# Latent attention: keys and queries projected by unrotated and rotated dimensions, not by halves of the heads

## The chip, the cores and the metric

One core of one Trainium2 chip runs the whole program. The time is that of one execution on the device in microseconds (us); lower is better. The kernel before was timed three times, and an execution of it was recorded by the hardware profiler.

## What is computed

The input is 16 sequences (batches) of 512 tokens with 256 features. After a layer norm, a state-space block (Mamba) and a transformer block run side by side and their outputs are added. The change lies in the transformer block's attention. It has 16 heads of 16 dimensions; the first 8 dimensions of each key and query head are unrotated, the last 8 are rotated by position:

```python
kv_lat = xn @ W_kvd                  # 256 -> 64
q_lat = xn @ W_qd                    # 256 -> 64
k = (kv_lat @ W_ku).reshape(B, S, NH, HH)          # NH = 16, HH = 8
q = (q_lat @ W_qu).reshape(B, S, NH, HH)
v = (kv_lat @ W_vu).reshape(B, S, NH, HD)          # HD = 16
q_rope = (q_lat @ W_ropeq).reshape(B, S, NH, HH)
k_rope = (xn @ W_ropek).reshape(B, S, NH, HH)
k_rope = k_rope * cos + rotate_half(k_rope) * sin
q_rope = q_rope * cos + rotate_half(q_rope) * sin
kk = jnp.concatenate([k, k_rope], axis=-1)
qq = jnp.concatenate([q, q_rope], axis=-1)
scores = jnp.einsum('bqhd,bkhd->bhqk', qq, kk) * scale      # causal, softmax
y = jnp.einsum('bhqk,bkhd->bqhd', probs, v).reshape(B, S, H)
return y @ W_o
```

Behind the attention come a residual sum, a norm, a shared expert and seven routed experts of which each token takes two.

## The kernel before

Three programs run one after the other on the core: `build_attn` (norm, attention, shared expert and routing, batch by batch), `build_experts` and `build_mamba`. The change touches `build_attn` and the host's weight layouts.

**Rounds and slots.** `build_attn` is a pipeline over batches. Every engine walks through one hand-written list, `ORDER`, once a round. The spine of the list is `S2_ITEMS`, 62 items (slots 0 to 61): transposed scores with their exponentials (`s2`), products with the values (`pv`), and copies of the outputs (`oc`). `AT` puts all other items in front of a slot: n, kind, i, j. `STAGE` says which batch an item works on: in round n, `s2` works on batch n, `s1` (scores for the row maxima) on n + 1, the projections (`T`, `lat`, `kq`, `split`, `mid`, `keep`, `stack`) on n + 2, and output projection, second norm and shared expert (`wo`, `h2`, `ht`, `route`, `g`, `u`) on n - 1. Rounds run from -3 on; ten of them lie in a hardware loop of five iterations with two rounds each, the others are written out. Engines execute their items in the list's order and wait for semaphores; a wait holds up all that stands behind it on the same engine or on SyncE's queue.

**Keys and queries.** `kq` items make float32 products of 512 columns in PSUM (PE L806 to L813). Group g holds the heads 8g to 8g + 7 with all 16 dimensions, laid out dimension first, so one tile of 128 rows has unrotated rows (0 to 63) and rotated rows (64 to 127). For each group: (g, 0) adds three products, the key up-projection from the latent and the two halves of the rotary key; (g, 1) is two products, the same with the halves of each rotated head exchanged; (g, 2) and (g, 3) are the query and the exchanged query, one product each. That is 7 a group, 14 a batch. DVE multiplies each bank by a table (`rope`, cosine or signed sine; 1 and 0 in the unrotated rows; L645, L647) into `ra` and `rb`, POOL adds them into `kq` (L492).

**Three bf16 parts.** Each group's key and query (128x1024) are split into three bf16 parts: `split` rounds on ACT (L581) and subtracts on POOL (L499), `mid` does the same again (L585, L506). `keep` stores the parts of a group in DRAM (L376, 768 KB), and `stack` (group 0, slots 36 to 43) and `stack1` (group 1, slots 1 to 8 of the next round) load them back as the operands `kst` and `qst`, six pairs of transfers of 128 KB a group (L385). `s1` of the first four head pairs waits for group 0's transfers, that of the last four for group 1's.

**Banks.** PSUM has rings of two banks each: X for `s2`, Y for `s1`, Z for every other product. A product waits until its bank has been read. DVE reads Y (row maxima, L619) and most of Z; ACT reads X (exponentials, L546).

**What stands near.** `wo` (slots 25 to 31, PE L910) needs `ym1`, POOL's multiplication of the outputs by the softmax shares (L510, slot 20). POOL ends `wo` with the sum `xs` (L520). SyncE's queue has, in this order: `xload` (18), `keep` 0 (30), `xrload` (33), the stack transfers of group 0 (36 to 43) with `so` between them (39), `sl` (43), `keep` 1 and `ro` (49), `rl` (53), `nmt` (56). `so`, `sl`, `ro`, `rl` take the softmax sums through DRAM; between `sl` and `ro` DVE makes a reciprocal (`rp`, slot 48, L666). DVE then has `u` (L756), the split of the row maxima (`nm`), the ranking (`rank`) and the second `g` (L752) before the transposes of the maxima on PE (`nmt`, slot 56, L889) find their bank free.

## Time and profile before

| | |
|---|---|
| median of 3 runs | 4080.77 us (4069.5 to 4081.09) |
| the profiled execution | 4091.09 us, span 4089.3 us |
| PE (matmul) busy | 3649.6 us, 89% |
| DVE busy | 2936.9 us, 72% |
| ACT busy | 2505.8 us, 61% |
| POOL busy | 2193.6 us, 54% |
| mean granted TensorE clock | 0.954 |

The page divides the span into 40 slices of 102 us and gives each engine's busy share in tenths. The attention program takes the first 14, the experts the next 5, the Mamba block the rest. A "granted clock" of 1.00 is 2.4 GHz and one of 0.50 is 1.2 GHz; a stretch's value is the mean. PE is the matmul engine, DVE the vector engine, ACT the scalar engine, POOL GpSimd, SPq the queue of SyncE, which issues the DMAs. A float32 product of 512 columns appears as two matmul records; matmuls are pipelined, so the duration of one includes its way through the array.

### The profile page before, as it was taken

The numbers are of one execution on the slowest core, as the hardware profiler recorded it, in microseconds if no ns is written. First come the engines' busy times: TensorE is split into PE (matmuls) and PEld (weight loads), VectorE is DVE, ScalarE is ACT, GpSimd is POOL, SyncE is SP. The second block draws the span as 40 slices with busy tenths as digits, with TensorE's granted clock in tenths as the row PEclk, the third lists the DMA queues.
The fourth block names the chain that finished last, engine by engine and source line by source line (L and its number), as shares of the span: only waits on it lengthen the run. The fifth ranks groups of instructions, "written<-read, shape, count | busy, mean of one in ns | idle before, by whom it ended". The sixth has DMA issues, their size and how long they took to land.

```text
span 4089.3 us, 70514 instructions
## 1 busy us (share of the span) xinstructions
PE 3649.6 (89%) x22264; PEld 2745.8 (67%) x22264; DVE 2936.9 (72%) x5456; ACT 2505.8 (61%) x6505; POOL 2193.6 (54%) x1115
## 2 busy tenths in 40 slices
PE   5999999999999659998799999999999999899987
PEld 2455555545554447777588888888888888888776
DVE  3566555565555122222699999999999999999997
ACT  1445444454444213332678788787888878888773
POOL 3244344334442200000487787877878788787774
PEclk8899999999999779999899999999999999999998
DMA  4333342333332157666222122221222222122221
GB/s 113 98 93 113 93 120 88 104 107 112 100 101 79 43 153 209 209 207 194 78 81 98 70 103 83 80 98 64 98 82 91 87 76 98 70 103 83 80 80 39
DMA packets 286369, 417.04 MB, mean 102 GB/s; under 512 B 78261, under 2 KB 250678, under 8 KB 263672
## 3 DMA queue, kind: packets, MB, share of 16 engines
q1 hardware_dynamic: 273048, 381.12, 29.2%
q0 software_dynamic: 12288, 33.57, 2.3%
q8 instruction: 106, 1.74, 0.2%
q10 hardware_dynamic: 864, 0.10, 0.0%
q14 instruction: 63, 0.52, 0.0%
HBM read 330.63 MB, written 83.17 MB: 101 GB/s over the span
## 4 chain that ended last, share of the span: by engine, by line
DVE 36%; issue 11%; PE 3%; ACT 2%; DVEq 1%; POOL 1%; DMA 0%; SPq 0%; ACTq 0%; POOLq 0%
DVE m_S L1760 8%; DVE m_PR L1760 8%; DVE m_S L1752 8%; DVE m_PR L1752 8%; DVE m_ub L1737 1%; ACT m_dA L1649 1%; DVE m_yz L1771 1%; DVE m_x L1721 1%; DVE m_th_x L1729 1%; DVEq L1751 1%; PE m_F L1870 1%; PE m_Y L1908 1%; POOL m_ub L1540 0%; PE m_F L1920 0%; PE m_F L1868 0%
## 5 line engine op out<-in xcount | busy, mean ns | idle before, releaser
L1540 POOL TENSOR_TENSOR m_ub<-m_Bb,m_dtx 128x2048 f32<-128x2048 f32 x254 | 1156.6, 4565 | 284.2 <-PE m_Y L1908 175.9
L1649 ACT ACTIVATE m_dA<-m_dt,m_a_neg 128x128 f32<-128x128 f32 x4096 | 1211.2, 388 | 135.0 <-DVE m_S L1760 134.6
L1908 PE MATMUL m_Y<-m_ub,m_ident 128*128 128x128 f32 x8192 | 956.3, 278 | 67.9 <-DVE m_ub L1737 67.6
L1908 PEld LDWEIGHTS m_Y<-m_ub,m_ident 128*128 128x128 f32 x8192 | 939.5, 194 | 79.2 <-DVE m_ub L1737 78.8
L546 ACT ACTIVATE f_pt<-f_X 128x512 f32<-128x512 f32 (+1 forms) x704 | 374.0, 557 | 512.8 <-PE f_X L843 506.7
L619 DVE TENSOR_REDUCE f_nm<-f_Y 128x1 f32<-128x512 f32 (+3 forms) x896 | 432.0, 531 | 249.4 <-PE f_Y L843 241.8
L1752 DVE SCALAR_TENSOR_TENSOR m_PR<-m_dA,m_S 128x512 f32<-128x512 f32 x512 | 355.8, 695 | 24.7 <-POOL m_ub L1540 6.3
L1752 DVE SCALAR_TENSOR_TENSOR m_S<-m_dA,m_PR 128x512 f32<-128x512 f32 x512 | 354.7, 693 | 12.0
L1760 DVE CUSTOM_DVE_ANT_1 m_S<-m_S,m_ub 128x512 f32<-128x512 f32 x512 | 352.8, 689 | 2.2 <-issue 2.2
L1760 DVE CUSTOM_DVE_ANT_1 m_PR<-m_PR,m_ub 128x512 f32<-128x512 f32 x512 | 352.9, 689 | 0.2 <-DVE m_PR L1752 0.2
L1737 DVE TENSOR_TENSOR m_ub<-m_S,m_Cb 128x512 f32<-128x512 f32 x512 | 349.7, 683 | 0.0
L1737 DVE TENSOR_TENSOR m_ub<-m_PR,m_Cb 128x512 f32<-128x512 f32 x512 | 349.7, 683 | 0.0
L1870 PE MATMUL m_F<-m_xpad,m_cv_diag 128*128 128x256 f32 x1024 | 285.1, 426 | 0.0
L1186 DVE SCALAR_TENSOR_TENSOR e_sg<-e_th,e_G 128x512 f32<-128x512 f32 x70 | 48.1, 688 | 326.9 <-ACT e_th L1130 326.9
L832 PE MATMUL f_X<-f_qst,f_kst 99*128 99x512 bf16 (+3 forms) x1024 | 250.4, 311 | 31.3 <-ACT f_pt L546 19.9
L826 PE MATMUL f_Y<-f_kst,f_qst 96*128 96x512 bf16 (+3 forms) x1024 | 236.0, 315 | 30.6 <-issue 15.8
L1491 POOL MEMSET m_ident<- 128x128 f32 x1 | 0.2, 204 | 472.7 <-POOLq L2037 472.7
L1870 PEld LDWEIGHTS m_F<-m_xpad,m_cv_diag 128*128 128x128 f32 x1024 | 201.4, 207 | 71.7 <-issue 45.5
L1844 PE MATMUL m_F<-m_xnT,m_w_in 128*128 128x256 f32 x1024 | 234.7, 383 | 3.1 <-DMA m_w_in<-L_attn_W_in 2.1
L1844 PEld LDWEIGHTS m_F<-m_xnT,m_w_in 128*128 128x128 f32 x1024 | 192.2, 193 | 28.2 <-DMA m_w_in<-L_attn_W_in 2.5
L510 POOL TENSOR_TENSOR f_yT<-f_yT,f_shares 128x1024 f32<-128x1024 f32 x32 | 75.1, 2348 | 250.2 <-DMA f_shares<-f_shares_dram 250.2
L859 PE MATMUL f_O<-f_pt,f_va 128*32 128x512 f32 (+3 forms) x2048 | 199.9, 464 | 2.7 <-ACT f_pt L546 2.7
(232 smaller groups left out, 6082.8 us busy)
## 6 DMA issues: line engine op xcount, KB each, us to landing
m_Bb<-m_bc_dram SPq DMA_DIRECT2D x64, 1024.0 KB, 4.8
m_Cb<-m_bc_dram SPq DMA_DIRECT2D x64, 1024.0 KB, 6.2
f_parts_dram<-f_parts SPq DMA_DIRECT2D x32, 768.0 KB, 3.7
f_kst<-f_parts_dram SPq DMA_DIRECT2D x192, 128.0 KB, 2.9
f_qst<-f_parts_dram SPq DMA_DIRECT2D x192, 128.0 KB, 3.1
e_rows<-sorted_rows SPq DMA_DIRECT2D x70, 256.0 KB, 2.8
e_wg<-Wg SPq DMA_DIRECT2D x70, 256.0 KB, 2.9
e_wu<-Wu SPq DMA_DIRECT2D x70, 256.0 KB, 4.1
```

Of the source, the lines that this page charges most:

```text
L546: act.activation(out, cols(bank_of(k, r)), func, **kw).then_inc(free_sem(k, r), 1)
L619: ins = dve.tensor_reduce(out, cols(full(k, r)), AX.X, ALU.max, negate=True)
L826: pe.matmul(bank[:, c0:c0 + n], qst[p][0:KS, h, qb * P:(qb + 1) * P], kst[p][0:KS, h, 0:n], start=(c0 == 0), stop=False, skip_group_check= ...
L832: pe.matmul(bank[:, c0:c0 + n], kst[p][:, h, kb * P:(kb + 1) * P], qst[p][:, h, kb * P:SEQ], start=(c0 == 0), stop=False, skip_group_check ...
L1540: pool.tensor_tensor(ub[:, h, i, :, :], Bb[:, s, :, :], dtx[:, m, None, s * SN:(s + 1) * SN].to_broadcast([P, NST, SN]), ALU.mult).then_in ...
L1649: last = act.activation(dA[:, h, i, n, :], dtt[:, par, m, s * SN:(s + 1) * SN], ACT.Exp, scale=a_neg[:, m, n:n + 1])
L1737: return dve.tensor_tensor(ub[:, h, 1:3, :, cols], state[:, :].rearrange("p (i n b) -> p i n b", i=2, n=NST), Cb[:, s, None, :, cols].to_b ...
L1752: dve.scalar_tensor_tensor(new, dA[:, h, :, :, cols].rearrange("p i n b -> p (i n) b"), DA_MIN, old, ALU.max, ALU.mult).then_inc(p_step, 1)
L1760: dve._custom_dve(bass.dve_ops.TENSOR_ADD_SAT, out=new, in0=new, in1=ub[:, h, 0:2, :, cols].rearrange("p i n b -> p (i n) b"), s0=CLIP, s1 ...
L1844: last = pe.matmul(F[(1 + i) % 4][:, m, :], w_in[:, k, blk * P:(blk + 1) * P], xnT[:, k, :], start=(k == 0), stop=(k == KM - 1))
L1870: last = pe.matmul(F[1 + i][:, j, :], cv_diag[:, k * MI + m, :], xpad[:, m, k * BATCH:k * BATCH + CN], start=False, stop=(k == TAPS - 1))
L1908: last = pe.matmul(Y[:, i * SN:(i + 1) * SN], ident[:, :], ub[:, h, 1 + i, n, :], start=False, stop=(n == NST - 1), skip_group_check=True)
```

## The change

The two tiles of 128 rows no longer hold eight heads each with all dimensions. Tile 0 holds the 8 unrotated dimensions of all 16 heads, tile 1 the 8 rotated ones.

- Tile 0: two products (64 rows each): keys from the latent, queries from the latent. ACT copies the two banks into `kq`; no multiplication, no addition.
- Tile 1: rotary keys (two products) and exchanged (two), rotary queries (one) and exchanged (one). DVE multiplies four banks, POOL adds two.
- In all 8 products in place of 14, 4 multiplications in place of 8, 2 additions in place of 4, and 2 copies on ACT. The weights `w_kra`, `w_krb` are half as large.
- The items move: `kq` to slots 14, 15, 17, 19, 21, 22 (none is left in slot 33), `split` to 18 and 26 (from 21 and 41), `mid` to 22 and 30 (from 26 and 45), `keep` to 26 and 34 (from 30 and 49).
- The tensor in DRAM has all 256 rows (dimension first, then head) of a part together. A transfer of `stack` or `stack1` still takes eight heads with 16 rows of 8 KB, but now reads rows that both `keep` transfers wrote. So the first transfer of either waits for both, and each `keep` waits for both stacks of the batch before.

```diff
@@ -46,10 +46,10 @@
...
-    w_kra = sb("f_w_kra", [P, KM, 2, P])
-    w_krb = sb("f_w_krb", [P, KM, 2, P])
+    w_kra = sb("f_w_kra", [P, KM, P])
+    w_krb = sb("f_w_krb", [P, KM, P])
...
-    w_ka = w_q[0:LAT, 0, :, :]
+    w_ka = w_q[0:LAT, 0, 0, :]
...
-    parts_dram = nc.dram_tensor("f_parts_dram", [2, PARTS, 2, P, SEQ], bf16).ap()
+    parts_dram = nc.dram_tensor("f_parts_dram", [PARTS, 2, 2 * P, SEQ], bf16).ap()
...
-                          (14, "kq", 0, 0), (16, "kq", 0, 1), (18, "kq", 0, 2), (18, "kq", 0, 3), (18, "xload", 0, 0), (20, "ym1", 1, 0),
-                          (20, "kq", 1, 0), (21, "split", 0, 0), (22, "kq", 1, 1), (25, "wo", 0, 0), (26, "mid", 0, 0), (27, "wo", 1, 0),
-                          (29, "wo", 2, 0), (30, "keep", 0, 0), (31, "wo", 3, 0), (33, "kq", 1, 2), (33, "kq", 1, 3), (33, "xrload", 0, 0), (34, "h2", 0, 0), (35, "h2a", 0, 0),
-                          (36, "stack", 0, 0), (37, "stack", 0, 1), (39, "stack", 0, 2), (40, "stack", 0, 3), (42, "stack", 0, 4), (43, "stack", 0, 5), (38, "ht", 0, 0), (39, "ht", 1, 0), (41, "split", 1, 0), (42, "route", 0, 0), (43, "route", 1, 0), (44, "lg", 0, 0),
-                          (45, "mid", 1, 0), (46, "g", 0, 0), (48, "xn", 0, 0), (49, "u", 0, 0), (49, "keep", 1, 0), (50, "nm", 0, 0), (52, "rank", 0, 0), (52, "g", 1, 0), (55, "u", 1, 0),
+                          (14, "kq", 0, 0), (15, "kq", 0, 1), (17, "kq", 1, 0), (18, "split", 0, 0), (18, "xload", 0, 0), (19, "kq", 1, 1), (20, "ym1", 1, 0),
+                          (21, "kq", 1, 2), (22, "kq", 1, 3), (22, "mid", 0, 0), (25, "wo", 0, 0), (26, "keep", 0, 0), (26, "split", 1, 0), (27, "wo", 1, 0),
+                          (29, "wo", 2, 0), (30, "mid", 1, 0), (31, "wo", 3, 0), (33, "xrload", 0, 0), (34, "keep", 1, 0), (34, "h2", 0, 0), (35, "h2a", 0, 0),
+                          (36, "stack", 0, 0), (37, "stack", 0, 1), (39, "stack", 0, 2), (40, "stack", 0, 3), (42, "stack", 0, 4), (43, "stack", 0, 5), (38, "ht", 0, 0), (39, "ht", 1, 0), (42, "route", 0, 0), (43, "route", 1, 0), (44, "lg", 0, 0),
+                          (46, "g", 0, 0), (48, "xn", 0, 0), (49, "u", 0, 0), (50, "nm", 0, 0), (52, "rank", 0, 0), (52, "g", 1, 0), (55, "u", 1, 0),
...
-                "T": [(kind, i)], "lat": [(kind,)], "kq": [(kind, i, j // 2, j % 2)],
+                "T": [(kind, i)], "lat": [(kind,)], "kq": [(kind, i, j)],
...
-                held(stacked[g], 16 * NSTACK * b)
+                held(stacked[0], 16 * NSTACK * b)
+                held(stacked[1], 16 * NSTACK * b)
...
-                sp.dma_start(parts_dram[g, :, :, :, :].rearrange("c n p t -> p (c n) t"),
+                sp.dma_start(parts_dram[:, :, g * P:(g + 1) * P, :].rearrange("c n p t -> p (c n) t"),
                              parts[:, g, :, :, :].rearrange("p c n t -> p (c n) t")).then_inc(parts_stored[g], 16)
...
                 if q == 0:
-                    held(parts_stored[g], 16 * (b + 1))
+                    held(parts_stored[0], 16 * (b + 1))
+                    held(parts_stored[1], 16 * (b + 1))
...
                 for n, (dst, part) in enumerate(((kst[p], K_PART[q]), (qst[p], Q_PART[q]))):
                     sp.dma_start(dst[q:KS:len(K_PART), g * 8:(g + 1) * 8, :].rearrange("d h t -> d (h t)"),
-                                 parts_dram[g, part, n, :, :].rearrange("(d h) t -> d (h t)", d=HD)).then_inc(stacked[g], 16)
+                                 parts_dram[part, n, :, :].rearrange("(d h) t -> d (h t)", d=HD)[:, g * 8 * SEQ:(g + 1) * 8 * SEQ]).then_inc(stacked[g], 16)
...
-            if kind == "kq" and j % 2 == 1:
+            if kind == "kq" and i == 1 and j % 2 == 1:
                 g, n = i, j // 2
-                pool.wait_ge(*used(("kq", g, n, 0), r))
-                pool.wait_ge(*used(("kq", g, n, 1), r))
+                pool.wait_ge(*used(("kq", g, j - 1), r))
+                pool.wait_ge(*used(("kq", g, j), r))
                 pool.wait_ge(hi_ready[g], b)
                 pool.wait_ge(rest_ready[g], b)
                 tt(kq[:, 2 * g + n, :], ra[:, n, :], rb[:, n, :], ALU.add).then_inc(kq_ready, 1)
@@ -494,7 +496,11 @@
                 g = i
                 pair = slice(2 * g, 2 * g + 2)
                 pool.wait_ge(hi_ready[g], b + 1)
-                pool.wait_ge(kq_ready, 4 * b + 2 * (g + 1))
+                if g == 0:
+                    pool.wait_ge(*used(("kq", 0, 0), r))
+                    pool.wait_ge(*used(("kq", 0, 1), r))
+                else:
+                    pool.wait_ge(kq_ready, 2 * (b + 1))
                 pool.wait_ge(lo_ready[g], b)
                 tt(kq[:, pair, :], kq[:, pair, :], parts[:, g, 0, :, :], ALU.subtract).then_inc(rest_ready[g], 1)
...
+            if kind == "kq" and i == 0:
+                act.wait_ge(lo_ready[0], b)
+                read(("kq", 0, j), kq[:, j, :], lambda bank: bank[:, :], ACT.Copy)
             if kind == "split":
                 g = i
-                act.wait_ge(kq_ready, 4 * b + 2 * (g + 1))
+                if g == 0:
+                    act.wait_ge(*used(("kq", 0, 0), r))
+                    act.wait_ge(*used(("kq", 0, 1), r))
+                else:
+                    act.wait_ge(kq_ready, 2 * (b + 1))
                 act.wait_ge(parts_stored[g], 16 * b)
                 act.activation(parts[:, g, 0, :, :], kq[:, 2 * g:2 * g + 2, :], ACT.Copy).then_inc(hi_ready[g], 1)
...
-            if kind == "kq":
-                g, n = i, j // 2
+            if kind == "kq" and i == 1:
+                n = j // 2
                 if j % 2 == 0:
-                    if not isinstance(b, int) or 4 * b + 2 * g + n >= 2:
-                        dve.wait_ge(kq_ready, 4 * b + 2 * g + n - 1)
-                    dve.tensor_tensor(ra[:, n, :], full(("kq", g, n, 0), r)[:, :], rope[:, 0, :], ALU.mult).then_inc(free_sem(("kq", g, n, 0), r), 1)
+                    if not isinstance(b, int) or b >= 1:
+                        dve.wait_ge(kq_ready, 2 * b + n - 1)
+                    dve.tensor_tensor(ra[:, n, :], full(("kq", 1, j), r)[:, :], rope[:, 0, :], ALU.mult).then_inc(free_sem(("kq", 1, j), r), 1)
                 else:
-                    dve.tensor_tensor(rb[:, n, :], full(("kq", g, n, 1), r)[:, :], rope[:, 1, :], ALU.mult).then_inc(free_sem(("kq", g, n, 1), r), 1)
+                    dve.tensor_tensor(rb[:, n, :], full(("kq", 1, j), r)[:, :], rope[:, 1, :], ALU.mult).then_inc(free_sem(("kq", 1, j), r), 1)
...
             if kind == "kq":
                 if isinstance(b, int) and b == 0:
                     pe.wait_ge(q_scaled, 1 + 16 * 2 * PARTS)
-                g, part = i, j % 2
-                if j == 0:
+                if i == 0 and j == 0:
                     pe.wait_ge(*used(("lat",), r))
                     pe.sem_inc(taken)
-                bank = free(("kq", g, j // 2, part), r)
-                if j == 0:
-                    pe.matmul(bank[:, :], w_ka[:, g, :], lat[0:LAT, :], start=True, stop=False)
+                bank = free(("kq", i, j), r)
+                if i == 0:
+                    w, rows_ = ((w_ka, lat[0:LAT, :]), (w_q[LAT:P, 0, 0, :], lat[LAT:P, :]))[j]
+                    last = pe.matmul(bank[:, :], w, rows_, start=True, stop=True)
+                elif j < 2:
+                    w = (w_kra, w_krb)[j]
                     for k in range(KM):
-                        last = pe.matmul(bank[:, :], w_kra[:, k, g, :], h1T[:, k, :], start=False, stop=(k == KM - 1))
-                elif j == 1:
-                    for k in range(KM):
-                        last = pe.matmul(bank[:, :], w_krb[:, k, g, :], h1T[:, k, :], start=(k == 0), stop=(k == KM - 1))
+                        last = pe.matmul(bank[:, :], w[:, k, :], h1T[:, k, :], start=(k == 0), stop=(k == KM - 1))
                 else:
-                    last = pe.matmul(bank[:, :], w_q[LAT:P, part, g, :], lat[LAT:P, :], start=True, stop=True)
-                full(("kq", g, j // 2, part), r, last)
+                    w = (w_q[LAT:P, 0, 1, :], w_q[LAT:P, 1, 0, :])[j - 2]
+                    last = pe.matmul(bank[:, :], w, lat[LAT:P, :], start=True, stop=True)
+                full(("kq", i, j), r, last)
...
-    c, s = (np.repeat(a.T, 8, axis=0) for a in (c, s))
+    c, s = (np.repeat(a.T[HH:], 16, axis=0) for a in (c, s))
...
+    def heads(w, swap=False):
+
+        w = w.reshape(-1, 16, 2, 4)
+        w = (w[:, :, ::-1, :] if swap else w).reshape(-1, 16, 8)
+        return w.transpose(0, 2, 1).reshape(-1, 128)
+    a['W_ka'] = heads(g['L0_ffn_W_ku'])
+    a['W_kra'] = heads(g['L0_ffn_W_ropek'])
+    a['W_krb'] = heads(g['L0_ffn_W_ropek'], True)
+    a['W_qa'] = np.concatenate([heads(g['L0_ffn_W_qu']), heads(g['L0_ffn_W_ropeq'])], axis=1)
+    a['W_qb'] = heads(g['L0_ffn_W_ropeq'], True)
```

## Rows read from the trace of the kernel before

**Rows 1.** The page's slices of PE, in tenths busy, 102 us each.

```profile
PE   5999999999999659998799999999999999899987
```

**Rows 2.** Stretches, busy us: PE, PEld, DVE, ACT, POOL; clock, DMA share, GB/s.

```profile
644.00:727.00 83.00, 80.57 (x504) 42.76 (x501) 49.91 (x127) 41.27 (x79) 35.43 (x35) 0.98 0.35 104
727.00:811.00 84.00, 79.48 (x473) 42.66 (x465) 46.77 (x117) 38.31 (x72) 31.26 (x33) 0.94 0.35 103
1060.00:1140.00 80.00, 77.67 (x493) 41.61 (x485) 48.67 (x123) 40.37 (x78) 33.91 (x34) 1.00 0.35 108
```

**Rows 3.** PE timeline, transposes of the maxima: start us, us, line, [idle before].

```profile
582.34 0.38 PE L889 MATMUL f_Z<-f_identb,f_nm_part 128*48 128x128 bf16 x4 [0.54 <-DVE f_sg L752]
...
749.65 0.38 PE L889 MATMUL f_Z<-f_identb,f_nm_part 128*48 128x128 bf16 x4 [0.55 <-DVE f_sg L752]
...
1001.77 0.38 PE L889 MATMUL f_Z<-f_identb,f_nm_part 128*48 128x128 bf16 x4 [0.52 <-DVE f_sg L752]
...
1161.37 0.38 PE L889 MATMUL f_Z<-f_identb,f_nm_part 128*48 128x128 bf16 x4 [1.02 <-DVE f_sg L752]
```

**Rows 4.** PE waits, 300 to 1200 us: total us, times, longest.

```profile
PE f_X L832 <- ACT f_pt L546: 11.0, 33, 0.5
```

**Rows 5.** PE in order of time, slots 14 to 25.

```profile
690.65 1.12 PE L806 MATMUL f_Z<-f_lat,f_w_q 64*128 64x512 f32 x2
691.70 1.98 PE L808 MATMUL f_Z<-f_h1T,f_w_kra 128*128 128x512 f32 x4
...
708.14 1.94 PE L910 MATMUL f_Z<-f_w_o,f_yT 128*128 128x256 f32 x8
```

**Rows 6.** PE in order of time, slots 33 to 35.

```profile
720.98 1.98 PE L813 MATMUL f_Z<-f_lat,f_w_q 64*128 64x512 f32 x4
722.89 0.39 PE L826 MATMUL f_Y<-f_kst,f_qst 96*128 96x512 bf16 x1
...
724.74 0.39 PE L826 MATMUL f_Y<-f_kst,f_qst 96*128 96x256 bf16 x2 [0.52 <-DVE f_nm L619]
```

**Rows 7.** DVE in order of time, the same stretch.

```profile
721.57 1.32 DVE L619 TENSOR_REDUCE f_nm<-f_Y 128x1 f32<-128x512 f32 x3
722.80 0.68 DVE L645 TENSOR_TENSOR f_ra<-f_Z,f_rope 128x512 f32<-128x512 f32 x1
```

**Rows 8.** Groups by line, 600 to 1000 us: busy, mean ns | idle before.

```profile
L492 POOL TENSOR_TENSOR f_kq<-f_ra,f_rb 128x512 f32<-128x512 f32 x20 | 25.3, 1264 | 46.9 <-issue 35.6 <-DVE f_rb L647 11.4
L499 POOL TENSOR_TENSOR f_kq<-f_kq,f_parts 128x1024 f32<-128x1024 f32 x10 | 21.3, 2125 | 31.9 <-ACT f_parts L581 31.9
...
L546 ACT ACTIVATE f_lat<-f_Z 128x512 f32<-128x512 f32 x5 | 3.0, 597 | 11.4 <-PE f_Z L795 11.4
```

**Rows 9.** POOL and the DMA queue in order of time, slots 20 to 43.

```profile
701.68 2.34 POOL L510 TENSOR_TENSOR f_yT<-f_yT,f_shares 128x1024 f32<-128x1024 f32 x1
...
723.55 2.36 POOL L520 TENSOR_TENSOR f_xs<-f_xn,f_xr 128x1024 f32<-128x1024 f32 x1
...
726.95 0.52 SPq L385 DMA_DIRECT2D f_kst<-f_parts_dram  x1
...
736.01 0.43 SPq L396 DMA_DIRECT2D f_sums<-f_sums_dram  x1
```

**Rows 10.** DMA issues, 300 to 1200 us: count, KB each, median us to landing.

```profile
f_parts_dram<-f_parts SPq DMA_DIRECT2D x21, 768.0 KB, 3.7
...
f_sums<-f_sums_dram SPq DMA_DIRECT2D x22, 16.0 KB, 1.9
```

**Rows 11.** DVE in order of time, slots 48 and 49.

```profile
741.36 0.34 DVE L666 RECIPROCAL f_sums<-f_sums 128x32 f32<-128x32 f32 x1
742.60 0.69 DVE L756 TENSOR_TENSOR f_sg<-f_sg,f_Z 128x512 f32<-128x512 f32 x1 [0.90 <-PE f_Z L946]
```

**Rows 12.** The first batch, in order of time.

```profile
46.44 0.37 SPq L376 DMA_DIRECT2D f_parts_dram<-f_parts  x1
...
59.85 0.59 PE L826 MATMUL f_Y<-f_kst,f_qst 96*128 96x512 bf16 x1 [15.76 <-issue]
```

24 lines of the change are left out of this document (6 added, 18 removed).

## The prediction

> **What bounds the kernel now.** I read the slices of the page first. TensorE is busy at nine tenths or more in nearly every slice of the first third, which is the attention program, the only part that the change touches; the experts and the Mamba part behind it issue the same instructions in both kernels [rows 1]. Then a table by stretches of about one round (a round is one pass of the order list, one batch of each stage): of 80 to 84 us PE is busy for 77.7 to 80.6, DVE for 47 to 50, ACT for 38 to 41 and POOL for 31 to 35 [rows 2]. The narrow transposes of the row maxima come once a round and so mark its length: 167.3 us for two rounds inside the loop (582.34 to 749.65), 159.6 past it (1001.77 to 1161.37) [rows 3]. Who waited for whom says the same: in the 900 us from 300 to 1200 PE waited 11.0 us for exponentials, its largest wait [rows 4]. So TensorE sets the pace of a round, and what leaves its queue comes off the end unless another engine is next. The next thing to look at is therefore each place where PE's cover gets thin.
>
> The profiled execution took 4091.1 us (span 4089.3), 10.3 us over the median 4080.8 of the runs shown. The savings below are worked out in the profiled execution and taken off the median.
>
> **TensorE.** A batch now has 14 projection products of 512 columns, each two records long. In the order list they stand in two places. Twelve stand in slots 14 to 22: three (690.65 and 691.70), two, two, and the same three and two again for the second group; wo's first product follows at 708.14 [rows 5]. The last two stand in slot 33, from 720.98 to the next instruction at 722.89, 1.91 us or 0.955 us a product [rows 6]. The single product with 64 rows at 690.65 takes 1.05 us to the next start, so fewer rows cost no less [rows 5]. After the change eight remain, all in slots 14 to 22: four of 0.91 to 0.96 us (two pairs, whose two records run without a gap) and four single ones of 0.96 to 1.05 us, together 7.5 to 8.0 us in place of 12 x 0.945 = 11.3 us. I take 7.7: 3.6 us less there. Slot 33 loses 1.91 us. PE's work falls by 5.5 us a batch.
>
> **Slot 33: the cover is partly lost.** DVE is the engine behind. After wo's last product it has the residual sum and statistics in its queue and reaches the row maxima of the next head only at 721.57 (1.32 us for three), then the two rotary multiplications of slot 33 from 722.80, then more maxima [rows 7]. PE had 1.91 us of products to do meanwhile and still waited 0.52 us for DVE at 724.74 [rows 6]. With the products gone PE stands ready for the next scores at 720.98 and finds both banks of its ring full; the first comes free when DVE has read 512 columns, at about 722.15. From there on DVE is rid of 1.37 us of multiplications, so the item that started at 724.74 starts at about 723.75. Of 1.91 us, 0.95 us is gained and 0.96 us turns into a wait. Sum so far: 3.6 + 0.95 = 4.55 us a round.
>
> **ACT, DVE, POOL.** DVE loses four multiplications of 0.68 us [rows 7] and POOL two additions of 1264 ns, ACT gains two copies of a bank, for which the row of the latent's copy stands, 597 ns [rows 8]. ACT and POOL have half a round idle [rows 2], so I cost the copies at nothing: each holds up one exponential by 0.6 us, in slots in which PE has a product of 0.95 us of its own to do. Without that cover they cost at most 2 x 0.6 us a round. POOL has one tight place. wo's first product needs the normalised heads, which POOL multiplies from 701.68 to 704.04 [rows 9]. Ahead of it stands now the remainder subtraction of the first group (2125 ns) and one addition (1264 ns) [rows 8]: taken from the start of slot 14 at 690.65 with PE's items moved up as above, the copies are done by 693.6, the bf16 rounding on ACT comes in its order at slot 18, about 697.1 to 698.2, then 2.1 us to 700.3, 1.3 us to 701.6, 2.35 us to 703.95. wo wants it at 708.14 - 3.6 = 704.5. Free, but by 0.5 us only; bounds 0 and 1.0 us a round.
>
> **SyncE's queue.** Both groups' parts must now have landed before the first stack transfer of slot 36, and that transfer blocks a queue that is served in order. Today the second group's parts are stored late (slot 49), and the stack begins at 726.95 as soon as the load of x that waits for POOL's sum of 723.55 (2.36 us) is out [rows 9]. After the change, that sum comes 3.6 us earlier, the load is issued at about 722.6 and the store of group 1 (keep, slot 34) at 723.3. The store alone takes 3.7 us to landing [rows 10]; right behind a load of 512 KB I allow up to 4.8, so the stack starts at 727.0 to 728.1, that is 0 to 1.2 us later than today on a clock where everything else is 4.55 us earlier. Queued behind are the other eleven stack transfers, the store of the softmax sums and then their load, which today is issued at 736.01, 9.06 us after the first stack transfer [rows 9]. That gives 736.2 to 737.3 for it, 1.9 us to landing [rows 10] and the reciprocal of 0.34 us on DVE [rows 11]: 738.5 to 739.6. DVE takes the reciprocal in its order, so whatever it waits stands before the u product's multiplication, which began at 742.60 after 0.90 us idle [rows 11] and would begin at 738.05. So DVE is late by 0.5 to 1.6 us, and behind it come the maxima's split, the ranking and the g product that frees the bank of the transposes, for which PE waited already (0.55 us at 749.65) [rows 3]: nothing covers it. I take 1.1 us, the middle. A page bears on the landing: the Trainium skill (DMA: Bandwidth & Descriptors, Anatomy of one DMA) gives a DMA about 2.0 us plus its bytes over 436 GB/s. By that, 512 and 768 KB in one queue would land 5.0 us after the first issue, 4.3 us after the second, and the wait would be about 1.1 us; with the 3.7 us of the row alone, 0.5 us. The range holds both.
>
> **The two ends.** In the first round PE waits for the stack. Today the first store is issued at 46.44 and PE starts scores at 59.85 [rows 12]. Eight products from 30.8 end at 38.4; with the last rotary multiplication, addition, two roundings of about 1 us and two subtractions of 2.1 us [rows 8] on engines that are also doing group 0, the second store is issued at about 48.4: 1.9 us lost, once. The second round holds no exponentials; there DVE's maxima are the bound and the saving lies between DVE's 2.8 us and PE's 5.5 us; I take 3.8, nearer to DVE's. The fourteen rounds after it hold a batch's projections each. The rounds without projections are as before.
>
> **Sum.** 14 x (4.55 - 1.1) = 48.3; + 3.8 - 1.9 = 50.2 us. 4080.8 - 50 = 4031 us.
>
> **The rivals.**
> A. All of PE's removed work comes off the end, since DVE also lost 2.8 us a batch and has a third of the round idle. 14 x 5.5 + 5.5 - 1.9 = 80.6: 4000 us. For it, PE's busy share [rows 2] and how little it waits [rows 4]. Against it, the DVE row at 721.57 and the reciprocal's place. 0.22.
> B. The clock. In the rounds of the loop the granted clock is 0.98 and 0.94 in turn, in a round past it 1.00 [rows 2], and two of those take 7.7 us less than two in the loop [rows 3]: PE falls from 2.4 to 1.2 GHz for a few us after its narrow products and idle stretches. More idle before the transposes and in slot 33 can make one more such fall a round, priced at the 0.98 row: 0.02 x 83 = 1.7 us lost. 14 x 1.7 = 24 us: 4055. It can go the other way too: without falls the ten rounds of the loop would get some 3 us each back, 4000. The Trainium skill (TensorE: Matmul & The Clock Gate, What's actually happening) has the clock halve after idleness and return with sustained work; the trace agrees, as the clock column of rows 2. 0.13.
> C. POOL's normalisation becomes the wait before wo: 1.0 us a round, 14 us more than forecast: 4045. For it, the margin of 0.5 us; against it, that POOL's chain starts from single products that now end earlier. 0.10.
> D. Slower. The stack's issues meet a queue in which the load and the store are still draining, and each takes twice its time: the load of the sums comes 9.06 us later still, and DVE is 10.2 us late in place of 1.1. It decides from a delay of 4.55 us on, where it has eaten the gain. 14 x (10.2 - 4.55) - 3.8 + 1.9 = 77 us slower: 4158. Against it, today's issues run at 9.06 us for the twelve and the store of the sums although the load of x drains just ahead of them [rows 9]. 0.05.
> E. Less than 0.3% either way (about what a measurement of this kernel can tell from no change), by C and B together with the 1.6 us end of the SyncE wait: 0.05.
>
> **How the numbers follow.** The forecast has 0.45. Faster by over 0.3%: 0.45 + 0.22 + 0.13 + 0.10 = 0.90; within: 0.05; slower: 0.05. The range goes from A and the better clock, 3996, to B and the upper ends, 4056.
>
> **What would show it.** PE's instructions: 16 x 6 x 2 = 192 matmul records fewer. A round of the loop about 3.5 us shorter, two of them 160.4 instead of 167.3. PE waiting for row maxima in slot 33 where nothing stood, about 1 us a round. DVE idle before the reciprocal of the sums, on its load, and PE's wait before the transposes of the maxima grown from 0.55 to about 1.6 us. The first scores at about 61.7. If instead PE waits before wo on POOL, C holds; if the reciprocal has no idle before it, A; if the clock column of the loop's rounds drops, B. The prediction is wrong if the second store lands before the queue wants it, or if the stack's issues stretch.

## The result, and the profile after

The changed kernel takes 4052.15 us, the median of 6 runs (4038.73 to 4057.35), against 4080.93 us for the kernel before in the same comparison, also 6 runs: a ratio of 0.9928 with a 95% interval of 0.9908 to 0.9947. So it is faster by 28.8 us, where 50 were forecast; the time lies inside the range, near its upper end. The profiled execution has a span of 4052.0 us.

The page of the changed kernel, its busy times and slices:

```profile
PE 3579.4 (88%) x22072; PEld 2713.9 (67%) x22072; DVE 2892.4 (71%) x5392; ACT 2521.9 (62%) x6537; POOL 2154.4 (53%) x1083
PE   4899999999998759998799999998999999999887
```

The slices look like those of [rows 1]: the difference is far too small for tenths. It can be seen in stretches that begin and end at the transposes of the row maxima. First the kernel before: up to the transposes of round -1, the first ones, then round 0, rounds 1 and 2, rounds 3 to 10, rounds 11 to 13, and round 14. The loop's code runs rounds 2 to 11, so "the eight rounds" (3 to 10) lie in it and have its four back edges among them; the two groups beside them have one loop round each (2 and 11) and no back edge. Columns as in [rows 2].

```profile
0.00:107.30 107.30, 60.27 (x185) 24.25 (x186) 43.25 (x97) 17.82 (x23) 39.69 (x66) 0.82 0.43 115
107.30:169.90 62.60, 59.20 (x356) 26.95 (x357) 36.95 (x91) 33.01 (x60) 17.19 (x18) 0.91 0.32 95
169.90:334.00 164.10, 156.80 (x950) 81.56 (x950) 91.98 (x225) 80.39 (x151) 59.37 (x58) 0.96 0.33 98
334.00:1001.80 667.80, 640.57 (x3881) 342.94 (x3882) 387.86 (x969) 319.70 (x601) 268.32 (x264) 0.96 0.35 103
1001.80:1242.00 240.20, 232.98 (x1455) 125.12 (x1456) 142.85 (x364) 119.39 (x226) 100.55 (x99) 0.99 0.35 106
1242.00:1314.50 72.50, 65.48 (x446) 36.36 (x446) 40.75 (x105) 32.45 (x65) 16.42 (x15) 0.95 0.23 70
```

The same stretches of the changed kernel:

```profile
0.00:99.50 99.50, 45.36 (x160) 18.78 (x160) 37.62 (x89) 20.00 (x27) 34.70 (x62) 0.80 0.42 110
99.50:160.80 61.30, 53.30 (x344) 24.86 (x345) 32.76 (x78) 34.46 (x63) 14.58 (x16) 0.91 0.40 114
160.80:331.30 170.50, 152.48 (x926) 79.69 (x927) 87.55 (x227) 82.23 (x154) 54.37 (x54) 0.92 0.32 94
331.30:974.10 642.80, 600.20 (x3785) 320.90 (x3786) 363.69 (x937) 327.39 (x616) 248.19 (x248) 0.96 0.36 107
974.10:1216.70 242.60, 227.74 (x1419) 122.77 (x1419) 137.38 (x351) 122.78 (x231) 93.04 (x93) 0.94 0.35 105
1216.70:1288.00 71.30, 64.19 (x445) 35.80 (x446) 40.68 (x105) 32.35 (x65) 16.44 (x15) 0.98 0.23 71
```

Behind each pair of times stands the length of the stretch. Up to the last transposes the attention program is 26.5 us shorter (1314.5 to 1288.0). The PE counts show where batches are projected: 25, 12, 24, 96, 36 and 1 records fewer, that is two batches in the first stretch, one in the second, then two, eight and three, and none in the last. The lengths show something that the forecast did not have: the eight rounds in the middle give 25.0 us, and the two rounds ahead of them and the three behind them are **longer** than before, by 6.4 and 2.4 us, although their PE work fell like that of the others. The clock column falls in just these (0.96 to 0.92, 0.99 to 0.94). The rest of the profiled difference of 37.3 us lies behind the last transposes, where the attention program ends and the experts and the Mamba part follow with the same instructions in both kernels; the profiled execution of before was itself 10.3 us over its median.

Who waited for whom on PE, us in total, times, longest. The kernel before, from 334 to 1001:

```profile
PE f_X L832 <- issue: 8.5, 4, 2.3
...
PE f_Z L889 <- DVE f_sg L752: 4.3, 8, 0.6
PE f_Y L826 <- DVE f_nm L619: 4.1, 8, 0.5
```

The changed kernel, the same eight rounds (331 to 974):

```profile
PE f_Z L903 <- DVE f_sg L766: 23.8, 8, 3.8
PE f_Y L840 <- DVE f_nm L632: 11.6, 16, 1.2
```

Two waits have grown, the one before the transposes (L903, formerly L889) from 0.54 to 2.98 us a round and the one for row maxima (L840, formerly L826) from 0.51 to 1.45. One is gone: 8.5 us in four places, each the first score behind the loop's back edge, in which PE waited for nothing that the profile shows.

One round of the changed kernel, SyncE's queue and DVE in order of time (the `xr` load, `keep` 1, the first stack transfer, the load of the sums, the reciprocal):

```profile
705.82 0.38 SPq L364 DMA_DIRECT2D f_xr<-x_tm  x1
706.59 0.37 SPq L377 DMA_DIRECT2D f_parts_dram<-f_parts  x1
713.45 0.52 SPq L387 DMA_DIRECT2D f_kst<-f_parts_dram  x1
...
721.75 0.42 SPq L398 DMA_DIRECT2D f_sums<-f_sums_dram  x1
723.87 0.35 DVE L680 RECIPROCAL f_sums<-f_sums 128x32 f32<-128x32 f32 x1 [3.50 <-DMA f_sums<-f_sums_dram]
```

The stack begins 6.86 us behind the store's issue. It is the store's landing that it waits for: by the trace this store took 6.6 us to land, and the load ahead of it 5.4. DVE idles 3.50 us before a reciprocal that had no wait in [rows 11]. PE in the same round: projections and wo's first product, slot 33, the transposes:

```profile
673.57 1.12 PE L820 MATMUL f_Z<-f_lat,f_w_q 64*128 64x512 f32 x2
...
687.69 1.56 PE L924 MATMUL f_Z<-f_w_o,f_yT 128*128 128x256 f32 x6
...
701.88 0.39 PE L840 MATMUL f_Y<-f_kst,f_qst 96*128 96x512 bf16 x1 [1.23 <-DVE f_nm L632]
...
731.12 0.38 PE L903 MATMUL f_Z<-f_identb,f_nm_part 128*48 128x128 bf16 x4 [3.08 <-DVE f_sg L766]
```

And the first batch (both stores, the first stack transfer, the first scores), to be read against [rows 12]:

```profile
41.68 5.72 SPq L377 DMA_DIRECT2D f_parts_dram<-f_parts  x2
50.79 0.56 SPq L387 DMA_DIRECT2D f_kst<-f_parts_dram  x1
...
60.55 0.59 PE L840 MATMUL f_Y<-f_kst,f_qst 96*128 96x512 bf16 x1 [23.17 <-issue]
```

### The profile page after: what moved, and what is told of

The parts are those of the page before. It is cut to its first block, busy times and chain, and to the rows that moved or that the text cites. A ratio compares the mean times of both kernels' runs of the same rounds, so it can differ in the third digit from the quotient of the medians.

```text
span 4052.0 us, 70010 instructions
## 1 busy us (share of the span) xinstructions
PE 3579.4 (88%) x22072; PEld 2713.9 (67%) x22072; DVE 2892.4 (71%) x5392; ACT 2521.9 (62%) x6537; POOL 2154.4 (53%) x1083
## 4 chain that ended last, share of the span: by engine, by line
DVE 36%; issue 11%; PE 2%; POOL 1%; DVEq 1%; ACT 1%; DMA 0%; SPq 0%; POOLq 0%; ACTq 0%
DVE m_S L1774 8%; DVE m_PR L1774 8%; DVE m_S L1766 8%; DVE m_PR L1766 8%; DVE m_ub L1751 2%; DVE m_yz L1785 1%; DVE m_x L1735 1%; POOL m_ub L1554 1%; DVEq L1765 1%; DVE m_th_x L1743 1%; ACT m_dA L1663 1%; PE m_F L1884 0%; PE m_Y L1922 0%; PE m_F L1858 0%; PE m_F L1934 0%
## 5 line engine op out<-in xcount | busy, mean ns | idle before, releaser
L840 PE MATMUL f_Y<-f_kst,f_qst 96*128 96x512 bf16 (+3 forms) x1024 | 236.8, 316 | 52.0 <-DVE f_nm L632 27.6
L846 PE MATMUL f_X<-f_qst,f_kst 99*128 99x512 bf16 (+3 forms) x1024 | 253.6, 317 | 27.3 <-ACT f_pt L552 19.2
L840 PEld LDWEIGHTS f_Y<-f_kst,f_qst 96*128 96x128 bf16 x1024 | 88.3, 102 | 186.2 <-issue 87.3
```

What stands on the lines that cost most here:

```text
L840: pe.matmul(bank[:, c0:c0 + n], qst[p][0:KS, h, qb * P:(qb + 1) * P], kst[p][0:KS, h, 0:n], start=(c0 == 0), stop=False, skip_group_check= ...
L846: pe.matmul(bank[:, c0:c0 + n], kst[p][:, h, kb * P:(kb + 1) * P], qst[p][:, h, kb * P:SEQ], start=(c0 == 0), stop=False, skip_group_check ...
```

## The experiments

Theory S: SyncE's queue. With both groups in one tensor, the store of group 1 stands before the stack, lands late behind the load of `xr`, and delays the sums, DVE and the transposes. Theory K: what is lost is lost to the clock, whatever the queue does. Theory D: in slot 33 PE waits for DVE, so its length is set there and not by PE. Theory P: PE sets the pace throughout. Theory H came out of the first batch's rows, where two products of 64 rows ran together. Theory C: the idle in slot 33 costs twice, once itself and once by the clock that falls behind it; N is its denial. Each ratio is against the kernel before, run on the same chip beside it.

**e1, the store ahead of the load.** The changed kernel, with `keep` 1 moved out from behind `xrload`.

```diff
-(31, "wo", 3, 0), (33, "xrload", 0, 0), (34, "keep", 1, 0), (34, "h2", 0, 0),
+(31, "wo", 3, 0), (32, "keep", 1, 0), (33, "xrload", 0, 0), (34, "h2", 0, 0),
```

> The changed kernel with one item moved: the store of group 1's parts goes to slot 32, ahead of the load of x in SyncE's queue, instead of slot 34 behind it. Theory S (the queue: store behind a 512 KB load, stack behind the store, softmax sums behind the stack, DVE behind the sums, PE's transposes behind DVE): in the changed kernel the store at 706.59 landed only when the stack could start at 713.45, the reciprocal waited 3.50 us at 723.87 and PE 2.13 us before the transposes. Now the store has landed before the load of x is out, the stack starts 0.7 us after the load, the reciprocal waits under 0.7 us, PE before the transposes about 0.5 to 0.9 us as before the change. 14 rounds x 1.5 us = 21 us off 4052, and some of the half-clock time with it: about 4028. Rival K (the clock and slot 33 have eaten the gain, the queue only fills idle that the others would make): within 6 us of 4052.

Measured: 4030.94 us (4024.1 to 4038.17), ratio 0.9871 (0.9852 to 0.989). SyncE's queue in one round: the load of `xr`, the first stack transfer, the load of the sums.

```profile
693.19 0.38 SPq L364 DMA_DIRECT2D f_xr<-x_tm  x1
693.98 0.53 SPq L387 DMA_DIRECT2D f_kst<-f_parts_dram  x1
...
702.91 0.42 SPq L398 DMA_DIRECT2D f_sums<-f_sums_dram  x1
```

The stack now follows the load by 0.8 us in place of 7.6, and the reciprocal waits for nothing; the stores of that round took 3.7 us each to land, and the load 4.4. PE's waits in its eight rounds (324 to 953):

```profile
PE f_Y L840 <- DVE f_nm L632: 11.6, 16, 1.2
...
PE f_Z L903 <- DVE f_sg L766: 4.8, 9, 0.5
```

The transposes are back at the wait of before, and S is shown: one item moved past its neighbour is worth 21 us by the medians, 23 by the ratios. The wait in slot 33 has not changed. Neither has the clock. PE around slot 33 of one round of e1:

```profile
689.25 0.39 PE L840 MATMUL f_Y<-f_kst,f_qst 96*128 96x512 bf16 x1 [1.24 <-DVE f_nm L632]
...
690.59 0.63 PE L846 MATMUL f_X<-f_qst,f_kst 99*128 99x512 bf16 x1
```

The stretch behind it, from e1's table by stretches, with the granted clock third from the end:

```profile
690.30:693.70 3.40, 3.40 (x18) 1.96 (x15) 1.99 (x6) 2.87 (x7) 2.50 (x3) 0.52 0.00 0
```

PE waits 1.24 us, works for 1 us, and then runs for 3.4 us at 1.2 GHz: the same score product takes 0.63 us in place of 0.38, with PE busy all the time. The same pair, wait and stretch, stands in each of the eight rounds of e1. [rows 2] had a round of the loop with a single such stretch and a stretch past 1060 with none. The changed kernel has the wait in all eight rounds too, but a half-clock stretch right behind it in only two of them (from 384 and from 947); behind the wait at 701.88, shown above, there is none:

```profile
702.50:706.50 4.00, 3.79 (x28) 1.65 (x29) 3.41 (x8) 3.15 (x8) 2.93 (x3) 1.00 0.00 0
```

**e2, each group's own store.** e1's cause by another road: the DRAM tensor and the waits of before come back, all else is as in the changed kernel.

```diff
-parts_dram = nc.dram_tensor("f_parts_dram", [PARTS, 2, 2 * P, SEQ], bf16).ap()
+parts_dram = nc.dram_tensor("f_parts_dram", [2, PARTS, 2, P, SEQ], bf16).ap()
...
-                held(stacked[0], 16 * NSTACK * b)
-                held(stacked[1], 16 * NSTACK * b)
+                held(stacked[g], 16 * NSTACK * b)
...
-                    held(parts_stored[0], 16 * (b + 1))
-                    held(parts_stored[1], 16 * (b + 1))
+                    held(parts_stored[g], 16 * (b + 1))
```

> The changed kernel with the tensor in DRAM and the waits of the kernel before: each group's stack reads only what its own store wrote and waits for that store alone. It leaves out the rearrangement (the rows that reach a head are not that head's), all instructions, sizes and transfers are the changed kernel's. Theory S: the stack starts right behind the load of x and the store of group 1, which it no longer waits for, so as in the run with the store moved ahead: reciprocal without a long wait, about 4028. Rival K: within 6 us of 4052. If this one gains and the moved store doesn't, it is not the landing of the store but the earlier wait on the transfers of the batch before.

Measured: 4018.28 us (4014.22 to 4023.49), ratio 0.9849 (0.9832 to 0.9865). That confirms S and goes some 9 us beyond e1, with intervals that overlap. By stretches (table below) the eight rounds agree with e1's within 4 us; most of the rest lies ahead of them. Whether it comes from the stack of group 0 no longer waiting for the store of group 1, or from each store waiting for one group's stack only, was not told apart.

**e3, the two products back in slot 33.** The changed kernel with two 64-row products (a query projection whose result nobody uses) where two stood before.

```diff
+            if kind == "kd":
+                for n in range(2):
+                    bank = free(("kd", n), r)
+                    last = pe.matmul(bank[:, :], w_q[LAT:P, 0, 1, :], lat[LAT:P, :], start=True, stop=True)
+                    full(("kd", n), r, last)
```

> The changed kernel with two products of 64 rows and 512 columns added in slot 33, where the kernel before had two; their results are thrown away (ACT reads four columns of each bank). It measures what the removal at that place was worth. Theory D (DVE's queue behind wo is the bound there; PE waited 1.24 + 0.21 us for row maxima at 623.15 and 623.81): 1.91 us of products fill 1.45 us of waiting, so 0.5 us a round, 4052 + 7 = 4059, and the waits there are gone. Rival P (PE is the bound everywhere): 14 x 1.91 = 27 us, 4079.

Measured: 4060.48 us (4048.32 to 4062.89), ratio 0.995 (0.9936 to 0.9964). Two products of one half take 1.9 us, as in [rows 6]; sixteen times that are 31 us of PE work, and the kernel is 8 or 9 us slower than the changed one, with intervals that overlap. D is right; P is not, for its 4079 lies above all runs. PE's waits in its eight rounds (322 to 963) show what pays:

```profile
PE f_Z L912 <- DVE f_sg L770: 21.0, 8, 3.4
PE f_X L855 <- ACT f_pt L553: 7.2, 22, 0.5
```

The wait for row maxima has left the list; that before the transposes, which hangs on SyncE, has hardly moved.

**e4, the two products of tile 0 side by side.** (0, 0) reads rows 0 to 63 of the array, (0, 1) rows 64 to 127.

```diff
-(14, "kq", 0, 0), (15, "kq", 0, 1), (17, "kq", 1, 0),
+(14, "kq", 0, 0), (14, "kq", 0, 1), (17, "kq", 1, 0),
```

> The changed kernel with the two unrotated products, keys (rows 0 to 63 of the array) and queries (rows 64 to 127), next to each other in slot 14 instead of 14 and 15. In the first two rounds, where no exponential item stands between them, the changed kernel shows both in 1.24 and 1.13 us (four records), where two products of the same rows took 1.91 us. Theory H (two products in different halves of the rows overlap): 0.8 us a round in the 14 full rounds, 11 us, about 4041. Rival (they overlap only where nothing follows, or ACT's two copies in a row then hold up the exponentials): 0 to 3 us.

Measured: 4042.29 us (4033.9 to 4045.24), ratio 0.9902 (0.9887 to 0.9918). One line holds both products, four records:

```profile
663.74 1.13 PE L820 MATMUL f_Z<-f_lat,f_w_q 64*128 64x512 f32 x4
664.80 0.39 PE L846 MATMUL f_X<-f_qst,f_kst 99*128 99x512 bf16 x1
```

Both take 1.06 us to the next start, as long as one alone (1.12 us at 673.57 above, two records). The forecast priced each at 0.955 to 1.05, one behind the other. The eight rounds became 15.6 us shorter, more than the 8 x 1.05 = 8.4 of the overlap; of the remainder 6 us stand in PE's wait before the transposes, which fell from 23.8 to 17.7; why it fell was not tested. As a whole time the gain is not clear of noise (the changed kernel's interval is 0.9908 to 0.9947); the overlap itself is read from the row. The Trainium skill (TensorEngine Tiling (Array Packing), Tiling Modes, Available Configurations and Key Properties) says that tiles operate independently and can load weights and multiply in parallel, and lists two of 64 x 128 among the configurations. The row agrees.

**e5, e1 with the two products in slot 33.** e1's edit and e3's together.

> The run with the store moved ahead of the load (4030.9 us), with two products of 64 rows added in slot 33, results thrown away. In that run every full round shows two stretches of 3.4 us at half clock: one begins about 10 us behind the first of slot 33's waits for DVE, one behind the narrow products of the router. Theory C (the wait in slot 33 costs twice: 1.45 us idle and 1.7 us by the clock that falls after it): the products cost 1.91 us, fill 1.45 us and save 1.7 us, so the kernel with more work is faster by 1.2 us a round, 4031 - 17 = 4014, and one of the two half-clock stretches is gone. Rival N (the clock falls there anyway, by the load around it): 0.5 us a round slower, 4038.

Measured: 4018.93 us (4011.13 to 4020.02), ratio 0.9838 (0.9815 to 0.9861). More work on the busiest engine, and the kernel is some 13 us faster than e1 by its ratio. The two intervals overlap a little, and e5 ran on another chip than e1, each beside the kernel before. What tells C from N is the clock of the eight rounds, 0.96 in e1:

```profile
324.80:939.60 614.80, 599.54 (x3816) 321.49 (x3817) 371.60 (x937) 329.26 (x633) 247.83 (x248) 0.99 0.38 112
```

628.3 us for the eight rounds have become 614.8. Read in windows of a quarter microsecond, e1 has 16 half-clock stretches there, eight right behind the wait in slot 33 and eight behind the router's narrow products; e5 has four, all behind the router's. C expected the first eight to go, N did not. (The expectation has the two mixed up: in e1 the stretch from 690.30 follows the wait within about 1 us; the one some 10 us behind it, at 700.5, is the router's.)

**e6, e1 and e4 together.**

```diff
+(14, "kq", 0, 0), (14, "kq", 0, 1), (17, "kq", 1, 0),
+(31, "wo", 3, 0), (32, "keep", 1, 0), (33, "xrload", 0, 0), (34, "h2", 0, 0),
```

> Both useful edits together on the changed kernel: the store of group 1 ahead of the load of x, and the two unrotated products side by side in slot 14 (alone 21 and 10 us). If the two savings are independent, as theory S and H have it (one on SyncE's queue, one in PE's own work): 4031 - 10 = 4021. If both only removed the same half-clock stretches: no better than 4031.

Measured: 4007.01 us (3989.32 to 4009.06), ratio 0.9803 (0.9776 to 0.9831), better than both alone and 14 us below the 4021 of two independent savings. In the eight rounds the two nearly add up (14.5 and 15.6 us alone, 31.9 together); where the rest of the 14 us comes from was not told apart, and e6 ran on another chip than e1 and e4. Here the clock differs from round to round: rounds of 75.0 us and of 77.1, with waits alike to half a microsecond.

**e7, e6 with the two products in slot 33.**

> The combination of moved store and side-by-side products, with the two 64-row products added in slot 33, results thrown away. Theory C: 17 us under the combination, about 4004. Rival N: 7 us over it, about 4028. The phase of the rounds differs from the run without the adjacent products, so it also tells whether the sign holds at another round length.

Measured: 3994.59 us (3987.95 to 4000.18), ratio 0.978 (0.9757 to 0.9803). **e8, e6 with a shorter filling**, six bf16 products of 512 columns on a constant, about 1.3 us:

```diff
+                    for q in range(3):
+                        last = pe.matmul(bank[:, :].rearrange("p (a s) -> p a s", s=P), identb[:, :], mask_k[:, None, :].to_broadcast([P, TT, P]),
+                                         start=(q == 0), stop=(q == 2))
```

> The same combination with a shorter filler in slot 33: six bf16 products of 512 columns (identity times a mask, about 0.22 us each, 1.3 us in all, results thrown away), which fit inside the 1.45 us that PE waits there. Theory C: the filler costs nothing and the half-clock stretch behind slot 33 goes, 14 x 1.7 = 24 us under the combination, about 3997. Rival N: within 3 us of the combination, about 4021.

Measured: 3999.22 us (3995.64 to 4002.61), ratio 0.9795 (0.9773 to 0.9817). The eight rounds of e6, from its table by stretches:

```profile
316.30:927.20 610.90, 584.31 (x3784) 317.46 (x3784) 373.11 (x937) 325.19 (x617) 248.09 (x248) 0.97 0.38 113
```

Those of e7:

```profile
317.50:918.40 600.90, 585.54 (x3816) 318.25 (x3817) 372.05 (x937) 327.34 (x633) 247.82 (x248) 1.00 0.39 115
```

e7 has 32 records more and is 10.0 us shorter: the clock column is at 1.00, with one half-clock stretch left of e6's ten. e8, with 49 records more, is 5.5 us shorter (605.4, at 0.99). The expectations counted from a combination of 4021 that came out at 4007. From there C says 3990 for e7 (3994.59 measured) and 3983 for e8 (3999.22), N 4014 and 4004 to 4010: e8 saves a third of what C priced, since a stretch stood behind slot 33 in only six of e6's eight rounds and e8 has five elsewhere. As whole times e6, e7 and e8 are not apart (their intervals overlap), so for C the runs give the direction in each of three pairs, and the traces the reason.

**e9, useful work in place of filling.** If the idle in slot 33 costs twice, the scores that wait there should come later, when DVE is through. Of e6, the two pairs of `s1` items around slot 33 go one slot down, `h2` and `h2a` as well; all work is useful.

```diff
-(33, "xrload", 0, 0), (34, "h2", 0, 0), (35, "h2a", 0, 0),
+(33, "xrload", 0, 0), (35, "h2", 0, 0), (36, "h2a", 0, 0),
...
-        AT.setdefault(2 + n * 47 // len(S1), []).append(item)
+        AT.setdefault({16: 34, 17: 36}.get(n, 2 + n * 47 // len(S1)), []).append(item)
```

> The combination of moved store and side-by-side products (4007 us), with real work in place of a filler: the scores and row maxima of slot 33 go to slot 34 and those of 35 to 36, the second norm's items of slots 34 and 35 one slot on. PE then has one exponential item of 0.28 us more to do before it needs the banks. Theory C: the wait of 1.24 us shrinks to about 1.0 us; that is 0.3 us a round, 4 us, and if the shorter wait also spares the half-clock stretch, up to 1.7 us more a round: between 3985 and 4003. Rival N, or the second norm's chain moved late so that PE waits at its transposes instead: 4007 to 4020.

Measured: 3990.68 us (3989.68 to 3994.37), ratio 0.9773 (0.9753 to 0.9794): 2.3% faster than the kernel before and 1.5 to 1.6% faster than the changed one. The wait at that place in one round of e9:

```profile
669.96 0.39 PE L840 MATMUL f_Y<-f_kst,f_qst 96*128 96x512 bf16 x1 [0.86 <-DVE f_nm L632]
```

0.86 us of the 1.24 are left, and six of the eight rounds keep the full clock: 599.7 us at 0.99, 11.2 us less than e6 with the same 3784 records. Against e6 as a whole time the gain is not clear of noise: the intervals overlap, and e9 ran on yet another chip.

All of them by stretch, from the table by stretches of each kernel (lengths in us, and the clock of the eight rounds):

| kernel | rounds 1 and 2 | rounds 3 to 10 | clock | rounds 11 to 13 |
|---|---|---|---|---|
| before | 164.1 | 667.8 | 0.96 | 240.2 |
| after | 170.5 | 642.8 | 0.96 | 242.6 |
| e1 | 163.7 | 628.3 | 0.96 | 239.9 |
| e2 | 160.3 | 624.6 | 0.96 | 236.6 |
| e3 | 163.1 | 640.9 | 0.97 | 245.3 |
| e4 | 164.0 | 627.2 | 0.96 | 241.4 |
| e5 | 159.9 | 614.8 | 0.99 | 235.2 |
| e6 | 155.7 | 610.9 | 0.97 | 235.7 |
| e7 | 158.2 | 600.9 | 1.00 | 232.2 |
| e8 | 159.1 | 605.4 | 0.99 | 231.9 |
| e9 | 155.0 | 599.7 | 0.99 | 229.4 |

## Why the prediction was partly right

The direction and the chain of waits were right. The length of a loop round came out too, but that is largely luck, as shown below. PE's transposes of the maxima in the changed kernel, two rounds apart:

```profile
490.27 0.59 PE L903 MATMUL f_Z<-f_identb,f_nm_part 128*48 128x128 bf16 x4 [3.48 <-DVE f_sg L766]
...
651.46 0.38 PE L903 MATMUL f_Z<-f_identb,f_nm_part 128*48 128x128 bf16 x4 [2.13 <-DVE f_sg L766]
```

That is 161.2 us, where 160.4 were forecast and 167.3 stood before [rows 3]. The gain was over-forecast by 21 us, and the stretches say where. Forecast and measured gain by stretch: to the first transposes 1.9 and 7.8 (the forecast's two ends lie in this one); round 0 3.45 and 1.3; rounds 1 and 2 6.9 and -6.4; rounds 3 to 10 27.6 and 25.0; rounds 11 to 13 10.35 and -2.4; round 14 0 and 1.2. Sum: 50.2 and 26.5.

**Slots 14 to 22.** Forecast 3.6 us less. From the first product to wo's it was 17.49 us [rows 5] and is 14.12 (673.57 to 687.69): 3.37. Right in mechanism, 0.2 short: the four single products cost 1.05 each, the upper end of the price.

**Slot 33.** Forecast: of 1.91 us, 0.95 gained. The wait grew by 1.45 - 0.51 = 0.94, so 0.97 was gained. The step is right to 0.02 us, and the trace has the wait where the text put it (1.23 us at 701.88). What the step left out is what the wait does to the clock: e1's rows show a new stretch at 1.2 GHz right behind it, and e5, e7 and e8 that it goes when the idle is filled. In the changed kernel it came in two of the eight rounds.

**SyncE's queue.** The right chain, link by link, with the first link mis-sized. Between store and stack 3.7 to 4.8 us were allowed; it took 6.86. The stack began 7.63 us after the load's issue, where 4.4 to 5.5 were forecast. The wait before the transposes grew by 2.98 - 0.54 = 2.44 us a round, where 1.1 were taken and 1.6 was the bound. The profile has the store's own landing, which was used [rows 10]; it did not show what a store meets behind a 512 KB load of the same queue. The Trainium skill's rule that the prediction quoted (DMA: Bandwidth & Descriptors, Anatomy of one DMA) gave 5.0 us from the first issue to the end of both; the trace has 0.77 + 6.6 = 7.4, so here it is 2.4 us too low. The section gives the rule for DMAs that GpSimd issues; these two are SyncE's. Why it takes so long was not tested.

**What the loop gave back.** By these terms a round would gain 3.37 + 0.97 - 2.44 = 1.9 us, yet 25.0 / 8 = 3.1 were measured. The rest is the stall behind the back edge, of which the forecast did not speak. PE in the kernel before, once in two rounds:

```profile
590.77 0.61 PE L832 MATMUL f_X<-f_qst,f_kst 99*128 99x512 bf16 x1 [2.06 <-issue]
```

The stretch around it, as a row by stretches:

```profile
590.00:597.00 7.00, 6.23 (x19) 4.04 (x20) 1.40 (x3) 1.79 (x3) 1.19 (x4) 0.51 0.55 139
```

Every second round PE stood for 1.89 to 2.30 us, and from the end of that stall on its clock was at half for some 7 us. In the changed kernel, and in e1, where no other wait could cover it, this stall is absent. 8.5 / 8 = 1.06 us a round brings the sum to 2.96. Round by round one sees that the agreement is luck. Rounds 6 (with a back edge) and 7 (without), first the kernel before, then the changed one:

```profile
582.30:668.50 86.20, 81.80 (x485) 43.73 (x485) 47.51 (x122) 40.13 (x76) 33.54 (x33) 0.94 0.34 100
668.50:749.60 81.10, 78.79 (x485) 42.05 (x485) 48.01 (x122) 39.78 (x76) 33.55 (x33) 0.98 0.36 107
...
570.70:651.50 80.80, 75.55 (x474) 40.11 (x475) 44.96 (x118) 40.85 (x77) 31.04 (x31) 0.96 0.36 106
651.50:731.10 79.60, 73.75 (x473) 39.70 (x474) 45.95 (x118) 40.89 (x77) 31.01 (x31) 0.98 0.37 109
```

One gained 5.4 us, the other 1.5. Of the 25.0 us of the eight rounds 20.6 stand in the four with a back edge (5.1 each) and 4.4 in the four without (1.1 each), where 3.45 were forecast for any. A queue wait 1.3 us longer than taken, and new clock falls, are hidden by a stall that went away.

The clock column is 0.96 in both kernels because falls changed places. Read in windows of a quarter microsecond, the eight rounds have 25.6 us lost to the clock in either, 15 falls of 1.7 us (a stretch of 7 us counts as two). Before, eight lie at the back edges and seven behind the router's narrow products. After, eight lie at the longer wait before the transposes, as in the row below (the wait of 3.48 us ends at 490.27), five behind the router's products and two behind slot 33.

```profile
489.50:497.00 7.50, 6.73 (x48) 2.97 (x49) 5.55 (x15) 3.10 (x6) 2.35 (x1) 0.54 0.12 44
```

Why the stall went is open; no experiment moved it alone.

**Rounds 1 and 2, and 11 to 13.** Here nothing cancelled: there is no back edge among them, and their clock had been up to 1.00 [rows 2]. It is not the loop's code that makes the difference, since rounds 2 and 11 run in it. The prediction's pair "past" the loop (1001.77 to 1161.37) begins with round 11, and of its 7.7 us on a pair in the loop 5.1 are the back edge (86.2 against 81.1 us). Time lost to the clock is length times one minus the clock column: 164.1 x 0.04 + 240.2 x 0.01 = 9.0 us before, 170.5 x 0.08 + 242.6 x 0.06 = 28.2 after, so 19 us. PE's idle (length minus busy) in the five rounds went from 14.5 to 32.9 us, 18.4 more, where the forecast's waits are 5 x 2.06 = 10.3. Together 19.2 + 8.1 = 27 us, against a shortfall of 10.35 + 2.4 + 6.9 + 6.4 = 26. So **rival B came true in part**: its price of 1.7 us for a fall was right, and falls did come at the two waits that it named, but not one more a round: these five rounds went from 5 falls to 16, the eight stayed at 15. Some of the added idle depends on what happened to fall together, as in round 12 of the changed kernel, which went from 80.0 to 84.4 us (wo's first product, DVE, PE in slot 33):

```profile
1090.37 3.51 PE L924 MATMUL f_Z<-f_w_o,f_yT 128*128 128x256 f32 x8 [1.33 <-POOL f_yT L516]
...
1108.04 0.18 DVE L705 BATCH_NORM_AGGREGATE f_mv<-f_st 128x2 f32<-128x6 f32 x1 [2.67 <-issue]
...
1108.85 0.61 PE L840 MATMUL f_Y<-f_kst,f_qst 96*128 96x512 bf16 x1 [3.84 <-DVE f_nm L632]
```

DVE stands for 2.67 us with nothing to wait for, and PE, without products in slot 33, waits it out. The kernel before had such stalls too (5.4 us in two places between 160 and 1001), each with PE work beside it. The first line is rival C's wait, once at 1.33 us between 300 and 1150, so the margin of 0.5 us held in the loop, and C as a case is wrong.

**The first batch.** Scores start at 60.55, 0.7 us later than before, where 1.9 were taken; the stretch up to the first transposes is 7.8 us shorter. It holds the second round as well, which gained 8.4 us where 3.8 were taken. In the kernel before, the last two products of that round took 3.78 us at half clock (90.92), twice the 1.98 of [rows 6]; and in both rounds two 64-row products of the changed kernel now run together (29.80 and 72.65, 1.24 and 1.13 us for four records), e4's effect by chance. **Rival A** is refuted by the waits on DVE, **D** by the queue: no issue was stretched, the twelve and the store of the sums still take 8.3 us (713.45 to 721.75).

The forecast of 4031 is what e1 measured (4030.94). That is no vindication: e1 is without the queue wait of 1.1 us a round which the forecast contained, and has the clock falls that it did not.

## What to carry to other kernels

When work comes off the engine that sets the pace, look at each place that it used to cover, and price an idle there twice: for itself, and for the clock that can fall behind it; then see whether work of a neighbouring slot can be put into the gap. When two buffers become one, the first reader inherits the latest writer: put that writer's store ahead of any large load in the same queue. And compare rounds one by one, those with a back edge apart from those without: a sum over rounds, or a pair of them, can agree with a forecast by errors that cancel.
